# Stores of the last two groups' v tiles moved from SyncE's queue to ScalarE's, with the first exponentials and one wait reordered

## The chip, the cores and the metric

The kernel runs on one core of a Trainium2 chip. The metric is the device time of one execution in microseconds (us). TensorE is PE in the profile, VectorE is DVE, ScalarE is ACT, GpSimd is POOL, SyncE is SP. SP computes nothing here: it waits for semaphores and issues DMAs.

## The reference, cut to what matters

One block of a gated cross-attention model. Eight batches of 128 tokens, width 512, 32 heads of width 128 (so q, k and v are 4096 wide), then a mixture-of-experts feed-forward. Only the attention matters for this change:

```python
x = _rmsnorm(hidden_states, ln_weight)
h_q = (x @ w_q.T).reshape(b, lq, H, DH)
h_k = (key_value_states @ w_k.T).reshape(b, lk, H, DH)
h_v = (key_value_states @ w_v.T).reshape(b, lk, H, DH)
score = jnp.einsum('bqhd,bkhd->bhqk', h_q, h_k) + position_bias[None]
score = jnp.where(m, score, -jnp.inf)
score = jax.nn.softmax(score, axis=-1)
score = jnp.where(m, score, 0.0)
attn = jnp.einsum('bhqk,bkhd->bqhd', score, h_v).reshape(b, lq, H * DH)
return hidden_states + attn @ w_out.T
```

All matrices are float32. Products that need it are made of three float32r products each, from a high and a low part of both sides (`three`, L798 to L805).

## The kernel before

**Stages.** (1) Projections of k and q, two heads a step, 32 steps (`project_seven`), written to DRAM as `kq`. (2) v of head groups 0 to 5, in 12 steps (`project_v_seven`), from PSUM by way of `st` to DRAM as `v_all`; a group is four heads, 512 columns. Steps alternate between `kq_stored[0]` and `kq_stored[1]`; the last step, STEPS - 1, counts on `kq_stored[1]`. (3) Attention, a loop over 32 heads, i from 0 to 31, with group g = i // 4. (4) The feed-forward.

**v of groups 6 and 7** is made inside stage 3, as work between the heads: 16 tiles m, 128 tokens by 512 columns each (`project_v(m)`, 12 matmuls of 128x512 into `ps_job[m % 2]`). ACT copies a tile to `v_out[:, m % 2]` (`take_v(m)`) and SP stores it to `v_all` (`keep_v(m)`, L544 to L546). `v_out` has two places, so the copy of tile m waits until the store of tile m - 2 has landed (`v_kept[m % 2]`), and `project_v(m)` waits until tile m - 2 has left PSUM (`v_sbuf` at m - 1). Tiles 0 to 4 (AHEAD) come ahead of head 0; FILL gives tiles 5 to 7 to head 0, 8 to 10 to head 1, 11 to 13 to head 2 and 14, 15 to head 3.

**PE's order in stage 3** (L1036 to L1052): `score(0)`, tiles 0, 1, 2, `score(1)`, tiles 3, 4, and then for each i `turn_probs(i)`, `score(i + 2)`, `attend(i)`, and the tiles of FILL (from head 4 on, output projections instead).

**One head** passes through the engines so: PE `score(i)` in two halves of four batches; DVE `bias_and_max(i)` adds POOL's `score_bias` and takes the row maximum; ACT `exps(i, half)`, four exponentials with row sums; DVE `normalise(i, half)`; PE `turn_probs(i)` transposes; ACT `take_pT(i)` copies the transposes to `pT`; PE `attend(i)`, whose matmuls read `pT` and `v_s`; ACT `take_attn_hi(i)` and DVE `take_attn_lo(i)` take the result from PSUM. All the order is written by hand: each engine has one program, and an instruction waits behind all that stand ahead of it.

**ACT's order around the change.** Ahead of its first tile stands `act.wait_ge(kq_stored[(STEPS - 1) % 2], stores(STEPS - 1))`: the stores of the last step of stage 2 must have landed, since `pT` lies where `st` was. Then tiles 0, 1, exps(0, 0), tiles 2, 3, exps(0, 1), tile 4, exps(1, 0), exps(1, 1), and in each head `take_pT(i)`, exps(i + 2, 0), `take_attn_hi(i)`, one tile, exps(i + 2, 1), the other tiles.

**SP's order** in the loop over heads: loads of k and q of head i + 2 (`load_kq`, behind score(i)), its position bias, for i = 0 the last group's weights (`load_wv_last(1)`), for i = 1 `load_v(1)` (2 MB), for i = 2 `load_wo(0)` (1 MB), and then the stores of the tiles made at that head: five for i = 0, three for each of the next three, two for i = 4.

Of the kernel before, what the change touches and what calls it, by code (L numbers as in the profile page):

```python
# [32 lines left out]
B = 8  # L33
# [61 lines left out]
def stores(s):  # L95

    return 16 * ((s // 2 + 1) if s < KQ else KQ // 2 + 2 * ((s - KQ) // 2 + 1))
# [8 lines left out]
def build(nc, x, ctxT, mask, gains, pbias, lnw, wa, wv, wo, sw12, sw3, ew12, eb12, ew3, rw, rb, b3, out):  # L106
    with ExitStack() as stack:
# [358 lines left out]
        def _(sp):  # L466
# [74 lines left out]
                    sp.wait_ge(wo_split, g)  # L541
                sp.dma_start(wo_raw[g % 2][:], wo[g]).then_inc(wo_in, 16)

            def keep_v(m):  # L544
                sp.wait_ge(v_sbuf, m + 1)
                sp.dma_start(v_all[2 * PAIRS + m // B, m % B], v_out[:, m % 2]).then_inc(v_kept[m % 2], 16)  # L546

            sp.wait_ge(const_done, 1)
            for s in range(KQ):
                if s + 2 < KQ:  # L550
# [27 lines left out]
            for i in range(H):  # L578
                g, j = divmod(i, G)
                if i + 2 < H:  # L580
                    sp.wait_ge(score_psum, 2 * (i + 1))
                    load_kq(i + 2)
                    sp.wait_ge(bias_ready, i + 1)
                    load_pos(i + 2)
                if i == 0:
                    sp.wait_ge(wv_last_split, 1)
                    load_wv_last(1)
                if i == 1:
                    load_v(1)
                if i == 2:  # L590
                    load_wo(0)
                if i < G:
                    for m in (AHEAD, FILL[0], FILL[1], FILL[2])[i]:
                        keep_v(m)
                if i == G:
                    for m in FILL[3]:
                        keep_v(m)
                if j == 1 and 0 < g < NG - 1:
                    sp.wait_ge(attn_psum, 2 * G * g)
                    load_v(g + 1)  # L600
                if j == 2 and g:
                    if g == 1:
                        sp.wait_ge(v_psum, 2 * B)
                    else:
                        sp.wait_ge(o_psum, B * (g - 1))
                    load_wo(g)
                if i == H - G + 1:
                    sp.dma_start(x_res[:], x.rearrange("t p d -> p t d")).then_inc(x_res_in, 16)
# [682 lines left out]
        def _(act):  # L1291
            act.dma_start(w_raw[0][:, 3], wa[0, :, 3]).then_inc(first_w_in, 16)

            def copy(dst, src):
                return nc.scalar.activation(dst, src, ACT.Copy)  # L1295
# [14 lines left out]
            def take_v(m):  # L1310
                act.wait_ge(v_psum, m + 1)
                if m >= 2:
                    act.wait_ge(v_kept[m % 2], 16 * (m // 2))
                copy(v_out[:, m % 2], ps_job[m % 2][:]).then_inc(v_sbuf, 1)

            def high_wv(u, k):
                block, j = ORDER[k], 7 * u + k - HI_PLACES
# [12 lines left out]
            def take_pT(i):  # L1330
                for half in range(2):
                    act.wait_ge(pT_psum, 2 * i + 1 + half)
                    copy(pT[:, half], ps_turn[half][:]).then_inc(pT_sbuf, 1)
# [124 lines left out]
                        for k in ((), (0,), (2,), (4, 5))[n]:  # L1458
                            high_wv(u + 1, k)

            act.wait_ge(kq_stored[(STEPS - 1) % 2], stores(STEPS - 1))
            for m in AHEAD:
                take_v(m)
                if m in (1, 3):
                    exps(0, m // 2)
            exps(1, 0)
            for i in range(H):
                g = i // G
                if i == 0:
                    exps(1, 1)  # L1470
                take_pT(i)
                if i + 2 < H:
                    exps(i + 2, 0)
                take_attn_hi(i)
                if g == 0:
                    take_v(FILL[i][0])
                if i + 2 < H:
                    exps(i + 2, 1)
                if g == 0:
                    for m in FILL[i][1:]:  # L1480
                        take_v(m)


            def split_w12(n):
# [652 lines left out]
```

## Time and profile before

| what | value |
|---|---|
| median of 3 runs | 984.06 us (982.69, 984.06, 2479.74) |
| profiled execution | 979.98 us, of which span 978.2 us |
| mean granted TensorE clock | 0.994 |
| PE busy | 943.2 us, 96% of the span |
| DVE, ACT, POOL busy | 643.6 us, 410.9 us, 280.4 us |
| DMA | 193.75 MB, mean 198 GB/s |

The profile is of one execution. The span is from its first to its last instruction; the time is 1.8 us longer. A row of the timeline gives the start in us from the span's start, the duration, the engine, the line and the tile, and in brackets how long the engine sat idle before it and what ended that. Ends of matmuls are modelled, so a matmul's busy time laps over the next one's; distances between starts are to be read. "issue" names idle time for which the profile shows no releaser.

### The profile page before, as it was taken

The page shows a single profiled execution, that of the slowest core. Times are in us where ns is not written, and L with a number is a line of the kernel's source. Part 1 is how long each engine was busy: PE and PEld are TensorE (multiplying, and loading weights), DVE is VectorE, ACT ScalarE, POOL GpSimd, SP SyncE. Part 2 cuts the span into 40 slices and gives each one's busy share as a digit, 9 for nine tenths or more (in the row PEclk, how much of TensorE's full clock was granted, in tenths as well). Part 3 has the DMA queues.
Part 4 walks back from the last instruction along what each step waited for, and adds up shares of the span by engine and source line. Part 5 has one row for each costly group of instructions (what it writes and reads, how often), then busy time and mean ns, then how long its engine had stood idle before and what let it go on. Part 6 is the DMA issues. An engine that isn't in the chain of part 4 may idle for free.

```text
span 978.2 us, 13972 instructions
## 1 busy us (share of the span) xinstructions
PE 943.2 (96%) x4843; PEld 786.7 (80%) x4843; DVE 643.6 (66%) x1068; ACT 410.9 (42%) x1004; POOL 280.4 (29%) x252
## 2 busy tenths in 40 slices
PE   7999999999999899997999999999999999989994
PEld 6888888888888688886889898988989887767772
DVE  6877679666665765643768777787787777843331
ACT  6236553333332342212655455554554425324442
POOL 1253424342433323002122222221221012043364
PEclk9999999999999999999999999999999999999998
DMA  7655554655547525637747737456365049565579
GB/s 267 212 198 180 191 186 151 226 194 182 211 166 250 202 111 191 216 134 261 274 157 286 244 108 265 166 193 221 133 226 184 38 180 334 201 205 175 173 181 253
DMA packets 86787, 193.75 MB, mean 198 GB/s; under 512 B 8608, under 2 KB 29344, under 8 KB 85312
## 3 DMA queue, kind: packets, MB, share of 16 engines
q1 hardware_dynamic: 79312, 177.67, 51.1%
q0 software_dynamic: 4784, 12.58, 5.6%
q10 hardware_dynamic: 2624, 2.62, 0.8%
q8 instruction: 40, 0.66, 0.3%
q14 instruction: 27, 0.22, 0.1%
HBM read 121.74 MB, written 71.11 MB: 197 GB/s over the span
## 4 chain that ended last, share of the span: by engine, by line
PE 59%; DVE 4%; DMA 1%; issue 1%; ACT 1%; another core or an unknown queue 0%; DVEq 0%; SPq 0%; ACTq 0%
PE ps_job L802 7%; PE ps_job L804 6%; PE ps_job L803 6%; PE ps_attn L1016 6%; PE ps_score L988 6%; PE ps_attn L1251 5%; PE ps_turn L1002 3%; PE ps_job L1260 3%; PE ps_turn L1235 1%; PE ps_attn L933 1%; PE ps_attn L932 1%; PE ps_attn L930 1%; DMA v_all<-st 1%; PE ps_score L930 1%; PE ps_score L933 1%; PE ps_score L932 1%
## 5 line engine op out<-in xcount | busy, mean ns | idle before, releaser
L726 POOL TENSOR_TENSOR score_bias<-mask_bias,pos_bias 128x1024 f32<-128x1024 f32 x32 | 78.0, 2436 | 300.2 <-DVE probs L1801 198.1
L1305 ACT ACTIVATE probs<-probs,neg_max 128x128 f32<-128x128 f32 x256 | 99.5, 392 | 97.4 <-DVE neg_max L1804 97.4
L685 POOL TENSOR_TENSOR w_sum<-w_raw 128x256 f32<-128x256 f32 x30 | 22.7, 758 | 179.6 <-PE ps_score L864 72.3
L1016 PE MATMUL ps_attn<-pT,v_s 128*128 128x128 f32 x512 | 62.6, 275 | 1.5 <-issue 1.2
L1251 PE MATMUL ps_attn<-ew_s,xbT 128*128 x248 | 62.1, 380 | 0.9 <-ACT xbT L1295 0.9
L988 PE MATMUL ps_score<-kq_s 128*128 128x128 f32 x512 | 62.4, 275 | 0.0
L1016 PEld LDWEIGHTS ps_attn<-pT,v_s 128*128 128x128 f32 x512 | 59.8, 192 | 1.9 <-issue 1.4
L1251 PEld LDWEIGHTS ps_attn<-ew_s,xbT 128*128 128x128 f32 x248 | 44.6, 190 | 20.4 <-issue 15.0
L988 PEld LDWEIGHTS ps_score<-kq_s 128*128 128x128 f32 x512 | 59.8, 192 | 0.2
L1801 DVE TENSOR_TENSOR probs<-ps_score,score_bias 128x512 f32<-128x512 f32 x64 | 43.7, 683 | 23.2 <-PE ps_score L988 20.6
L1828 DVE TENSOR_TENSOR acc<-ps_job,acc 128x512 f32<-128x512 f32 x56 | 37.9, 686 | 29.6 <-PE ps_job L804 29.6
L758 POOL DMA_INDIRECT xb<-x_rows,token_of x31 | 31.2, 1008 | 85.5 <-ACT y_out L1557 38.1
L1295 ACT ACTIVATE w_hi<-w_sum 128x1024 fp32r<-128x1024 f32 x30 | 31.8, 1061 | 53.1 <-POOL w_sum L690 53.1
L1295 ACT ACTIVATE w_hi<-w_raw 128x768 fp32r<-128x768 f32 (+3 forms) x38 | 31.2, 822 | 54.0 <-PE ps_score L864 24.0
L1295 ACT ACTIVATE pT<-ps_turn 128x512 f32<-128x512 f32 x64 | 34.5, 592 | 45.6 <-PE ps_turn L1002 45.6
L802 PE MATMUL ps_job<-wo_hi,attn_even_lo 128*128 128x512 f32 x128 | 51.2, 400 | 0.0
L1648 DVE TENSOR_TENSOR w_lo<-w_raw,w_hi 128x768 fp32r<-128x768 f32 (+1 forms) x31 | 41.0, 1323 | 14.6 <-ACT w_hi L1295 14.2
L804 PE MATMUL ps_job<-wo_hi,attn_even_hi 128*128 128x512 f32 x128 | 50.0, 391 | 0.0
L803 PE MATMUL ps_job<-wo_lo,attn_even_hi 128*128 128x512 f32 x128 | 49.9, 389 | 0.0
L1305 ACT ACTIVATION_READ_ACCUMULATOR probs<-probs,neg_max 128x1 f32 x256 | 48.8, 191 | 0.0
L1815 DVE TENSOR_TENSOR probs<-probs,row_scale 128x512 f32<-128x512 f32 x64 | 44.3, 692 | 2.2
L1804 DVE TENSOR_REDUCE neg_max<-probs 128x4 f32<-128x512 f32 x64 | 43.9, 686 | 2.2
(465 smaller groups left out, 2596.6 us busy)
## 6 DMA issues: line engine op xcount, KB each, us to landing
kq<-st SPq DMA_DIRECT2D x32, 1024.0 KB, 4.2
kq_s<-kq SPq DMA_DIRECT2D x64, 512.0 KB, 4.5
v_s<-v_all SPq DMA_DIRECT2D x8, 2048.0 KB, 10.8
w_raw<-wa_dram SPq DMA_DIRECT2D x31, 512.0 KB, 5.6
v_all<-st SPq DMA_DIRECT2D x24, 512.0 KB, 3.7
y_slots<-ones SPq DMA_DIRECT2D x32, 256.0 KB, 4.7
wo_raw<-wo_dram SPq DMA_DIRECT2D x8, 1024.0 KB, 6.8
ew_s<-ew_dram SPq DMA_DIRECT2D x4, 2048.0 KB, 12.8
```

Source lines behind the costliest of these rows:

```text
L726: nc.gpsimd.tensor_tensor(score_bias[:], mask_bias[:], pos_bias[:, i % 2].unsqueeze(1).broadcast_to([P, B, P]), ALU.add).then_inc(bias_rea ...
L802: nc.tensor.matmul(psum, l_lo, r_hi, start=(k == 0), stop=False)
L803: nc.tensor.matmul(psum, l_hi, r_lo, start=False, stop=False)
L804: last = nc.tensor.matmul(psum, l_hi, r_hi, start=False, stop=(closed and k == n - 1))
L988: last = nc.tensor.matmul(ps_score[half][:, cols(b)], kq_s[:, i % 2, 1, tok], kq_s[:, i % 2, 0, tok], start=True, stop=True)
L1016: last = nc.tensor.matmul(ps_attn[half][:, cols(b)], v_s[g % 2][:, BH * half + b, cols(j)], pT[:, half, cols(b)], start=True, stop=True)
L1251: last = nc.tensor.matmul(ps_attn[k][:, 0:2 * P], xbT[k][:, cols(c)], ew12_s[:, e, c], start=(c == 0), stop=(c == C - 1))
L1295: return nc.scalar.activation(dst, src, ACT.Copy)
L1305: last = nc.scalar.activation(probs[i % 2][:, half, b], probs[i % 2][:, half, b], ACT.Exp, bias=neg_max[:, i % 2, half, b:b + 1], accum_ou ...
L1801: V.tensor_tensor(probs[i % 2][:, half], ps_score[half][:].rearrange("p (b k) -> p b k", b=BH), score_bias[:, BH * half:BH * (half + 1)], ...
L1804: V.tensor_reduce(neg_max[:, i % 2, half], probs[i % 2][:, half], AX.X, ALU.max, negate=True)\
L1815: V.tensor_tensor(probs[i % 2][:, half], probs[i % 2][:, half], row_scale[:, half].unsqueeze(2).broadcast_to([P, BH, P]), ALU.mult).then_i ...
```

## The change

SP's `keep_v` and its calls go. `take_v` on ACT now waits for its own copy and issues the store itself. The wait for `kq_stored[1]` moves behind the five tiles ahead, to just before the first `take_pT`. The exponentials stand otherwise: exps(0, 0) behind tile 1 and exps(0, 1) behind tile 2, exps(1, 1) behind `take_pT(0)`, exps(2, 0) behind tile 5 and exps(2, 1) behind tile 7. Two waits for all stores stand ahead of `take_attn_hi(6)`.

```diff
-            def keep_v(m):
-                sp.wait_ge(v_sbuf, m + 1)
-                sp.dma_start(v_all[2 * PAIRS + m // B, m % B], v_out[:, m % 2]).then_inc(v_kept[m % 2], 16)
...
-                if i < G:
-                    for m in (AHEAD, FILL[0], FILL[1], FILL[2])[i]:
-                        keep_v(m)
-                if i == G:
-                    for m in FILL[3]:
-                        keep_v(m)
...
                 copy(v_out[:, m % 2], ps_job[m % 2][:]).then_inc(v_sbuf, 1)
+                act.wait_ge(v_sbuf, m + 1)
+                act.dma_start(v_all[2 * PAIRS + m // B, m % B], v_out[:, m % 2]).then_inc(v_kept[m % 2], 16)
...
-            act.wait_ge(kq_stored[(STEPS - 1) % 2], stores(STEPS - 1))
             for m in AHEAD:
                 take_v(m)
-                if m in (1, 3):
-                    exps(0, m // 2)
+                if m in (1, 2):
+                    exps(0, m - 1)
             exps(1, 0)
+            act.wait_ge(kq_stored[(STEPS - 1) % 2], stores(STEPS - 1))
             for i in range(H):
                 g = i // G
+                take_pT(i)
                 if i == 0:
                     exps(1, 1)
-                take_pT(i)
-                if i + 2 < H:
+                elif i + 2 < H:
                     exps(i + 2, 0)
+                if i == G + 2:
+
+                    for n in range(2):
+                        act.wait_ge(v_kept[n], 16 * B)
                 take_attn_hi(i)
                 if g == 0:
                     take_v(FILL[i][0])
-                if i + 2 < H:
+                if i == 0:
+                    exps(2, 0)
+                elif i + 2 < H:
                     exps(i + 2, 1)
                 if g == 0:
                     for m in FILL[i][1:]:
                         take_v(m)
+                if i == 0:
+                    exps(2, 1)
```

ACT's program before, from its first copy of a v tile (`probs_73` is `probs` of even heads, `probs_74` of odd ones; each pair of `probs` rows is one exps of four exponentials):

```order
L1295 ACTIVATE v_out<-ps_job 128x512 [waits v_psum,kq_stored1]
L1295 ACTIVATE v_out<-ps_job 128x512 [waits v_psum]
L1305 ACTIVATE probs_73,row_sum<-probs_73,neg_max 128x128 [waits max_done]
L1305 ACTIVATE probs_73,row_sum<-probs_73,neg_max 128x128 x3
L1295 ACTIVATE v_out<-ps_job 128x512 [waits v_kept0,v_psum]
L1295 ACTIVATE v_out<-ps_job 128x512 [waits v_kept1,v_psum]
L1305 ACTIVATE probs_73,row_sum<-probs_73,neg_max 128x128 [waits max_done]
L1305 ACTIVATE probs_73,row_sum<-probs_73,neg_max 128x128 x3
L1295 ACTIVATE v_out<-ps_job 128x512 [waits v_kept0,v_psum]
L1305 ACTIVATE probs_74,row_sum<-probs_74,neg_max 128x128 [waits max_done]
L1305 ACTIVATE probs_74,row_sum<-probs_74,neg_max 128x128 x3
```

ACT's program now, from the same place up to the copy and store of tile 3 (L1285 is now the line of the copy helper, L1306 the store's):

```order
L1285 ACTIVATE v_out<-ps_job 128x512 [waits v_psum]
L1306 DMA v_all<-v_out 128x512 [waits v_sbuf]
L1285 ACTIVATE v_out<-ps_job 128x512 [waits v_psum]
L1306 DMA v_all<-v_out 128x512 [waits v_sbuf]
L1295 ACTIVATE probs_73,row_sum<-probs_73,neg_max 128x128 [waits max_done]
L1295 ACTIVATE probs_73,row_sum<-probs_73,neg_max 128x128 x3
L1285 ACTIVATE v_out<-ps_job 128x512 [waits v_kept0,v_psum]
L1306 DMA v_all<-v_out 128x512 [waits v_sbuf]
L1295 ACTIVATE probs_73,row_sum<-probs_73,neg_max 128x128 [waits max_done]
L1295 ACTIVATE probs_73,row_sum<-probs_73,neg_max 128x128 x3
L1285 ACTIVATE v_out<-ps_job 128x512 [waits v_kept1,v_psum]
L1306 DMA v_all<-v_out 128x512 [waits v_sbuf]
```

The first copy no longer waits for `kq_stored1`, and a DMA stands behind each copy. Behind tile 7, at the end of head 0, ACT went straight to the copies to `pT` of head 1 before:

```order
L1295 ACTIVATE v_out<-ps_job 128x512 [waits v_kept0,v_psum]
L1295 ACTIVATE v_out<-ps_job 128x512 [waits v_kept1,v_psum]
L1295 ACTIVATE pT<-ps_turn 128x512 [waits pT_psum] x2
L1305 ACTIVATE probs_74,row_sum<-probs_74,neg_max 128x128 [waits max_done]
L1305 ACTIVATE probs_74,row_sum<-probs_74,neg_max 128x128 x3
```

Now the store of tile 7 and exps(2, 1) stand between:

```order
L1285 ACTIVATE v_out<-ps_job 128x512 [waits v_kept0,v_psum]
L1306 DMA v_all<-v_out 128x512 [waits v_sbuf]
L1285 ACTIVATE v_out<-ps_job 128x512 [waits v_kept1,v_psum]
L1306 DMA v_all<-v_out 128x512 [waits v_sbuf]
L1295 ACTIVATE probs_73,row_sum<-probs_73,neg_max 128x128 [waits max_done]
L1295 ACTIVATE probs_73,row_sum<-probs_73,neg_max 128x128 x3
L1285 ACTIVATE pT<-ps_turn 128x512 [waits pT_psum] x2
```

The two exponential rows there are exps(2, 1), which stood behind tile 5 before. SP's queue before, from the loads of head 2 (i = 0) to the stores of head 1:

```order
L522 DMA kq_s<-kq 128x1024 [waits kq_stored1,score_psum]
L522 DMA kq_s<-kq 128x1024
L525 DMA pos_bias<-pbias_dram 128x128 [waits bias_ready]
L516 DMA wv_last_raw_72<-wv_dram 128x2048 [waits wv_last_split]
L546 DMA v_all<-v_out 128x512 [waits v_sbuf] x5
L522 DMA kq_s<-kq 128x1024 [waits kq_stored1,score_psum]
L522 DMA kq_s<-kq 128x1024
L525 DMA pos_bias<-pbias_dram 128x128 [waits bias_ready]
L537 DMA v_s_61<-v_all 128x8x512 [waits v_in,kq_stored1,kq_stored0]
L546 DMA v_all<-v_out 128x512 [waits v_sbuf] x3
```

And now:

```order
L522 DMA kq_s<-kq 128x1024 [waits kq_stored1,score_psum]
L522 DMA kq_s<-kq 128x1024
L525 DMA pos_bias<-pbias_dram 128x128 [waits bias_ready]
L516 DMA wv_last_raw_72<-wv_dram 128x2048 [waits wv_last_split]
L522 DMA kq_s<-kq 128x1024 [waits kq_stored1,score_psum]
L522 DMA kq_s<-kq 128x1024
L525 DMA pos_bias<-pbias_dram 128x128 [waits bias_ready]
L537 DMA v_s_61<-v_all 128x8x512 [waits v_in,kq_stored1,kq_stored0]
L522 DMA kq_s<-kq 128x1024 [waits kq_stored0,score_psum]
```

The loads that stood behind five and then three stores now wait for the scores alone. PE's, DVE's and POOL's programs are unchanged.

## Rows read from the trace of the kernel before

**Rows 1.** Waits of PE from 439 us on: total us, times, longest.

```profile
PE ps_job L802 <- ACT v_out L1295: 5.2, 1, 5.2
...
PE ps_attn L1016 <- issue: 1.2, 1, 1.2
...
PE ps_turn L1002 <- DVE probs L1815: 0.2, 1, 0.2
```

**Rows 2.** Chain that ended last, 435 to 500 us: start, duration, what.

```profile
440.95 10.60 DMA v_all<-st
```

**Rows 3.** Timeline of ACT: start, duration, line, tile, idle before.

```profile
451.57 1.09 ACT L1295 ACTIVATE v_out<-ps_job 128x512 f32<-128x512 f32 x2 [13.92 <-DMA v_all<-st]
...
464.01 0.60 ACT L1295 ACTIVATE v_out<-ps_job 128x512 f32<-128x512 f32 x1 [0.59 <-PE ps_job L804]
...
466.04 0.39 ACT L1305 ACTIVATE probs<-probs,neg_max 128x128 f32<-128x128 f32 x1
...
467.58 1.06 ACT L1295 ACTIVATE pT<-ps_turn 128x512 f32<-128x512 f32 x2
...
478.51 0.60 ACT L1295 ACTIVATE v_out<-ps_job 128x512 f32<-128x512 f32 x1 [2.12 <-PE ps_job L804]
479.00 1.08 ACT L1295 ACTIVATE pT<-ps_turn 128x512 f32<-128x512 f32 x2
```

**Rows 4.** Timeline of PE, same columns: tiles ahead, head 0, head 1.

```profile
446.59 0.39 PE L804 MATMUL ps_job<-wv_last_hi,ctx_hi 128*128 128x512 f32 x1
452.22 0.79 PE L802 MATMUL ps_job<-wv_last_hi,ctx_lo 128*128 128x512 f32 x1 [5.24 <-ACT v_out L1295]
...
456.55 1.95 PE L988 MATMUL ps_score<-kq_s 128*128 128x128 f32 x16
458.25 0.47 PE L802 MATMUL ps_job<-wv_last_hi,ctx_lo 128*128 128x512 f32 x1
...
463.81 0.60 PE L1002 MATMUL ps_turn<-ident,probs 128*128 128x128 f32 x4
...
468.26 2.02 PE L1016 MATMUL ps_attn<-pT,v_s 128*128 128x128 f32 x16 [1.21 <-issue]
470.04 0.47 PE L802 MATMUL ps_job<-wv_last_hi,ctx_lo 128*128 128x512 f32 x1
...
478.31 1.03 PE L1002 MATMUL ps_turn<-ident,probs 128*128 128x128 f32 x8
...
480.97 1.95 PE L1016 MATMUL ps_attn<-pT,v_s 128*128 128x128 f32 x16
482.67 0.48 PE L802 MATMUL ps_job<-wv_last_hi,ctx_lo 128*128 128x512 f32 x1
```

**Rows 5.** Busy time by stretch: each engine, granted clock, DMA share, GB/s.

```profile
452.00:454.00 2.00, 1.78 (x4) 1.49 (x5) 0.00 (x0) 2.00 (x10) 0.00 (x0) 0.50 1.05 420
...
456.00:458.00 2.00, 2.00 (x17) 1.87 (x16) 0.29 (x1) 0.00 (x0) 0.00 (x0) 1.00 0.54 200
```

**Rows 6.** Tile v_out: the issues of its stores (ns), and issue to landing.

```profile
L546 SPq DMA_DIRECT2D v_all<-v_out x16: 319/320/327, 452.2 to 514.3; - x16
...
DMA to landing us min/median/max: 2.0/2.2/6.4
```

**Rows 7.** Timeline of SP's queue, 425 to 515 us.

```profile
441.56 1.11 SPq L522 DMA_DIRECT2D kq_s<-kq  x2
...
452.19 12.76 SPq L546 DMA_DIRECT2D v_all<-v_out  x5
...
466.50 0.37 SPq L537 DMA_DIRECT2D v_s<-v_all  x1
```

**Rows 8.** Line L522, the two loads issued from 441.6 us: issue to landing.

```profile
DMA to landing us min/median/max: 11.2/11.5/11.9
```

**Rows 9.** Line L1420, a 256 KB load on ACT's queue: issue (ns), landing.

```profile
L1420 ACTq DMA_DIRECT2D lnw_s<-lnw_dram x1: 477/477/477, 34.9 to 34.9; - x1
...
DMA to landing us min/median/max: 4.9/4.9/4.9
```

## The prediction

> **What bounds the kernel now.** I read the page first: PE is busy 96% of the span. So a change in ACT's program counts only where PE waits for ACT. The waits of PE from 439 us on, the start of stage 3, show few [rows 1]: one of 5.2 us for a copy to `v_out`, one of 1.2 us ahead of `attend(0)`, 0.2 us ahead of the second half of `turn_probs(0)`. The chain says what is behind the first: a store `v_all<-st` that takes 10.6 us to land, until 451.55 [rows 2]. ACT starts its first copy of a v tile at 451.57, after 13.9 us of idleness [rows 3], since it waits for `kq_stored[1]` first, though `v_out` has nothing to do with `st`. PE, with tiles 0 and 1 finished at 446.82 (446.59 and one matmul of 0.23), stands until 452.22 [rows 4]. Then it pays again: the granted clock is 0.50, the level of 1.2 GHz, from 452 to 454 us, and 1.00 from 456 on [rows 5]; tile 2 takes 456.55 - 452.22 = 4.33 us, where tiles 5 to 7 take (478.31 - 470.04) / 3 = 2.76 each [rows 4].
>
> Head 0 is slow as well. From the end of tile 4 to the first tile behind `attend` PE takes 470.04 - 463.81 = 6.23 us; in head 1 the same work takes 482.67 - 478.31 = 4.36 [rows 4]. The 1.87 us between come from exps(0, 1) and from exps(1, 0) and (1, 1), which stand ahead of `take_pT(0)`: copy of tile 4 at 464.01, copies to pT at 467.58 [rows 3].
>
> **The first wait goes: what it gives.** Tile 0 ends at about 446.82 - 2.76 = 444.06. Its copy now starts 0.20 later (the distance of 463.81 and 464.01, and of 478.31 and 478.51 [rows 3, 4]), long before PE asks for `ps_job[0]` at 446.82. PE then runs on: tile 2 to 449.58, `score(1)` for 1.70 (456.55 to 458.25) to 451.28, tiles 3 and 4 for 5.56 (458.25 to 463.81) to 456.84 [rows 4]. Before, it was 463.81: **6.97 us gained**, of which 5.40 is the standstill and 1.57 the slow clock (4.33 - 2.76).
>
> **What that rests on: store 0.** Copy 2 waits for store 0, and tile 4 waits for copy 2. Tile 4 would start at 456.84 - 2.78 = 454.06, and PE follows the start of a copy by 0.65 (451.57 to 452.22), so store 0 may land up to 453.4. It is issued 0.62 after the start of its copy (451.57 to 452.19 [rows 3, 7]), so at about 444.9, and has 8.5 us. Landing takes 2.2 us at the median and 6.4 at most, the latter for the stores issued at 452.2 behind all that SP had queued [rows 6, 7]. But at 444.9 more is queued than at 452.2: the transfers that SP has issued by then keep the DMA engines full (share 1.05, 420 GB/s) until 456 or so [rows 5], and the two issued at 441.56 took 11.2 and 11.9 us [rows 7, 8]. If ACT's queue is served beside SP's, store 0 (256 KB) lands in 2.2 to 5 us, which is the 4.9 us that a 256 KB load on ACT's queue took [rows 9]; if it is served in the order of issue over both queues, it lands where it lands now, at 452.2 + 6.4 = 458.6. The trace has no case that tells these apart; I take the first, since the rows of ACT's own queue are nearest, and keep the second as a rival.
>
> The Trainium skill (DMA: Bandwidth & Descriptors, Queues, rings and completion order) says that SP and ACT each have a ring of their own on every DMA engine and that an engine goes round its rings packet by packet. By that rule store 0 passes the backlog, and the sum is as here; the 4.9 us of rows 9 agree but do not prove it. The same page (Issuing engines are not separate DMA queues) says that issuing from several engines saves only the sequencer's issue time; read strictly it speaks against this change and would give the time of the late store below.
>
> Stores 1 to 4 have more room: copy 3 waits for store 1 (issued at 447.6) and matters to tile 5 after 462; copy 5 waits for store 3 by 465.
>
> **What the stores cost ACT.** Each take_v now ties up ACT for longer: 0.62 from the copy's start to the issue, then the issue itself, 0.32 (SP, the same transfer [rows 6]) to 0.48 (ACT's queue [rows 9]). I take 0.40: the next instruction starts 1.02 behind the copy's start instead of 0.49 (478.51 to 479.00 [rows 3]). Sixteen times 0.53 is 8.5 us, nearly all under ACT's idleness; it counts where pT waits. There are two such places.
>
> - Head 0. From the end t of tile 4: copy t + 0.20, store to t + 1.22, exps(1, 0) 4 x 0.385 (466.04 to 467.58 [rows 3]) to t + 2.76, `pT`, and `attend(0)` 0.68 later (467.58 to 468.26 [rows 3, 4]) at t + 3.44. PE is ready at t + 2.66 (478.31 to 480.97). It waits 0.78; the 0.42 ahead of it goes, as exps(0, 1) ends at about 452.4 now and DVE has normalised by 457. Head 0 takes 4.36 + 0.78 = 5.14 instead of 6.23: **1.09 gained**.
> - Head 1. exps(2, 1) now stands between store 7 and `take_pT(1)`: the same 3.44 against 2.66, where no wait was: **0.78 lost**.
>
> With the issue at 0.32 or 0.48 each wait is 0.70 or 0.86. Heads 2 and 3 have a store but no exps ahead of pT: t + 1.90, hidden.
>
> **Edits at nothing.** The moved wait: its store landed at 451.55, and pT is not wanted before 459. If it were later by 1.9 us (three stores of 256 KB at 420 GB/s) it would still be hidden; queued behind it are the copies to pT. The waits at head 6 are for stores some 25 us old; behind them stand `take_attn_hi(6)` and all ACT does, but nothing is late. SP's loads come sooner: `load_v(1)`, issued at 466.50 before [rows 7], now follows `score(1)`, at about 453. The loads of k and q for head 2 landed by 441.56 + 11.9 = 453.5 [rows 7, 8], plus 1.9 is 455.4, and `score(2)` wants them after 456.84: hidden by 1.4 us or more. Behind head 4 nothing changes, and PE has no other waits for ACT there, so what is gained stays to the end.
>
> **Sum.** 6.97 + 1.09 - 0.78 = 7.28 us. The profiled execution took 979.98 us (span 978.2 and 1.8 around it): **972.7**. The median of the runs shown lies 4.08 above the profiled one: 984.06 - 7.28 = **976.8**, which I predict. Extreme prices: with both waits of pT at 0.86, 0.16 less gain; with neither, 8.84 us, or 975.2. Further down is only the scatter between executions, up to 4.08 us.
>
> **The rivals**
> - **Late store.** Store 0 lands at 458.6. Copy 2 and tile 4 (459.2) come then; PE has stood 5.2 us, nearly as now, and pays the slow clock: tile 4 ends at 459.2 + 4.33 = 463.6 instead of 463.8. The stall has only moved from tile 2 to tile 4. Gain 0.2 + 0.31 = 0.5 us: 983.5. For: full DMA engines. Against: rows 9, and 8.5 us of room. Anything between gives 977 to 983.
> - **Starved stores, slower.** If ACT's queue gets nothing while SP's has work, the earlier loads hurt: 1 MB for head 3 and the 2 MB of `load_v(1)`, issued by 453 into a queue that is not yet empty. At 420 GB/s they take 7.3 us: store 0 lands at 465.9, tile 4 starts at 466.5 and ends at 470.8, 7.0 later than before. Less 0.31 that is 6.7 us slower: 990.8. It decides from a landing at about 459 on. Against: again rows 9, a load on ACT's queue amid SP's traffic.
> - **Dear issues.** If an issue on ACT takes two or three times 0.48, each of the two waits grows by 0.5 to 1.0: 978 to 979. Or the loads for `score(2)` slip past 456.84 by 1 or 2 us: the same times.
>
> **Numbers.** The case forecast 0.74, late store or in part 0.15, starved 0.03, dear issues or late loads 0.08. The range 972 to 983.5 leaves out the starved case and part of the scatter; the forecast's own is 973 to 979. A measurement of this kernel tells about 2%, 20 us, from no change; no case reaches that. Faster by over 2% 0.01, within 2% 0.98, slower by over 2% 0.01.
>
> **What would show it.** Right: ACT's first copy near 444.3; PE without a gap between tiles 1 and 4; granted clock 1.00 from 440 to 460; store 0 landing in under 8.5 us; gaps of about 0.8 us ahead of `attend(0)` and `attend(1)`; the first `turn_probs` near 456.8; ACTq issues of 0.3 to 0.5 us. Wrong: a PE gap ahead of tile 4 (late store), ahead of `score(2)` (late loads), gaps well over 0.8 ahead of the attends (dear issues), or a loss behind head 4.

## The result and the profile after

The kernel after takes 978.63 us at the median of 9 runs (977.05 to 980.71); the kernel before, run beside it, 983.0 (one of its nine runs took 2479.74 us and is left out of the ratio). The ratio is 0.9957, with a 95% interval of 0.9949 to 0.9966: about 4.4 us faster, where 7.28 were forecast. 978.63 lies in the range of 972.0 to 983.5, 1.8 us above the 976.8 predicted. That distance flatters the forecast: 976.8 was counted down from 984.06, the median of the first three runs of before. From 983.0, the median of all nine, 7.28 less is 975.7, and the kernel after is 2.9 us above that. The profiled execution took 978.93 us (span 977.2, mean granted clock 0.990), only 1.05 us less than the profiled execution of before; the reason is told below.

**The first wait is gone, as forecast.** PE's timeline of after, as in [rows 4]:

```profile
455.96 1.04 PE L992 MATMUL ps_turn<-ident,probs 128*128 128x128 f32 x8
...
462.65 2.90 PE L1006 MATMUL ps_attn<-pT,v_s 128*128 128x128 f32 x16 [3.86 <-issue]
...
474.34 1.03 PE L992 MATMUL ps_turn<-ident,probs 128*128 128x128 f32 x8
...
477.73 2.05 PE L1006 MATMUL ps_attn<-pT,v_s 128*128 128x128 f32 x16 [0.56 <-ACT pT L1285]
...
487.81 1.04 PE L992 MATMUL ps_turn<-ident,probs 128*128 128x128 f32 x8
```

The first `turn_probs` starts at 455.96 instead of 463.81. Measured from the start of `score(0)`, which came 0.82 us earlier in this execution, it is 17.20 us instead of 24.23: 7.03 gained, 6.97 forecast. The granted clock is 1.00 from 440 to 462 us. But `attend(0)` now waits 3.86 us, and `turn_probs(1)` is 474.34 - 455.96 = 18.38 us behind `turn_probs(0)`, where it was 14.50 before [rows 4] and 13.41 was forecast. Head 1, from `turn_probs(1)` to `turn_probs(2)`, takes 13.47 instead of 12.63. From there on the two kernels run alike: from `turn_probs(2)` to the last one it is 297.84 us before and 297.86 after. The waits of PE from 435 us on (total, times, longest; the first and fifth row of the view), as in [rows 1]:

```profile
PE ps_attn L1006 <- issue: 3.9, 1, 3.9
...
PE ps_attn L1006 <- ACT pT L1285: 0.8, 2, 0.6
```

**What `attend(0)` waits for.** "issue" names no releaser. ACT's timeline of after, as in [rows 3], shows it:

```profile
443.48 0.60 ACT L1285 ACTIVATE v_out<-ps_job 128x512 f32<-128x512 f32 x1 [6.64 <-PE ps_job L794]
444.11 0.35 ACTq L1306 DMA_DIRECT2D v_all<-v_out  x1
...
451.71 0.60 ACT L1285 ACTIVATE v_out<-ps_job 128x512 f32<-128x512 f32 x1 [2.85 <-DMA v_all<-v_out]
452.33 0.33 ACTq L1306 DMA_DIRECT2D v_all<-v_out  x1
...
454.27 0.58 ACT L1285 ACTIVATE v_out<-ps_job 128x512 f32<-128x512 f32 x1
454.88 0.33 ACTq L1306 DMA_DIRECT2D v_all<-v_out  x1
459.43 0.60 ACT L1285 ACTIVATE v_out<-ps_job 128x512 f32<-128x512 f32 x1 [4.58 <-DMA v_all<-v_out]
...
461.98 1.05 ACT L1285 ACTIVATE pT<-ps_turn 128x512 f32<-128x512 f32 x2
```

ACT's first copy is at 443.48 and store 0 is issued at 444.11. Copy 2 waits 2.85 us for that store to land, which costs PE nothing. Store 2, issued at 452.33, goes out of the same place of `v_out`. Copy 4, at 459.43, waits 4.58 us for it. exps(1, 0) and the copies to `pT` (461.98) stand behind copy 4 on ACT, and `attend(0)` follows at 462.65. PE had tile 4 done at 455.96, and ACT would have started copy 4 at 456.16 (0.20 later): it is 3.27 us late. With the 0.56 us of wait that head 1 shows without a late copy, that is 3.83 of the 3.86. Tile v_out of after, as in [rows 6]: the issues of its stores, and the landings of all 16:

```profile
L1306 ACTq DMA_DIRECT2D v_all<-v_out x16: 326/326/347, 444.1 to 511.2; - x16
...
DMA to landing us min/median/max: 2.0/4.0/7.5
```

Line L1306 of after, store 0 alone:

```profile
DMA to landing us min/median/max: 7.5/7.5/7.5
```

The same line, store 2 alone:

```profile
DMA to landing us min/median/max: 7.0/7.0/7.0
```

The median of 16 is 4.0 us, against 2.2 before; the first took 7.5 and the third 7.0. And the standstill costs a second time, as the first one did in [rows 5]. Stretches of after: each engine, granted clock, DMA share, GB/s:

```profile
460.00:462.00 2.00, 0.00 (x0) 0.00 (x0) 0.00 (x0) 1.60 (x10) 0.00 (x0) 1.00 1.06 403
462.00:464.00 2.00, 1.35 (x10) 1.38 (x11) 1.03 (x3) 2.00 (x9) 0.00 (x0) 0.90 1.05 406
464.00:466.00 2.00, 2.00 (x10) 1.90 (x9) 1.33 (x4) 1.46 (x6) 0.00 (x0) 0.50 1.06 410
466.00:468.00 2.00, 2.00 (x8) 1.55 (x8) 1.93 (x4) 0.19 (x1) 0.23 (x1) 0.75 1.05 413
```

PE does nothing from 460 to 462; the clock then is 0.50, the level of 1.2 GHz, from 464 to 466, and partly so on both sides. Head 0 takes 18.38 us where 13.41 were forecast, 4.97 more. By distances between starts, `attend(0)` is 6.69 us behind `turn_probs(0)`, where 3.44 were forecast: 3.25 more for the wait. From there to `turn_probs(1)` it is 11.69 us, where 9.97 were forecast: 1.72 more for the slow clock (the same work takes 10.08 in head 1).

**The two profiled executions differ elsewhere too.** Their 1.05 us are 0.82 ahead of `score(0)`, 2.29 in stage 3 (from `score(0)` to the last head's `turn_probs`, 349.20 to 346.91), and 2.1 lost behind it (189.4 to 191.5 us), where the change touches nothing. The last goes with a fall of the granted clock near 850 us, to 0.86 from 850 to 860 and 0.96 in the 10 us before. The kernel before shows such a fall too, in two further profiles of itself. Stretch of before_again:

```profile
850.00:860.00 10.00, 9.37 (x43) 7.38 (x43) 4.60 (x11) 3.05 (x7) 4.32 (x4) 0.83 1.04 391
```

The same 10 us of the first profile of before (the execution whose rows the prediction reads), with the clock at 1.00:

```profile
850.00:860.00 10.00, 9.31 (x50) 7.54 (x51) 6.14 (x14) 3.06 (x7) 4.31 (x4) 1.00 1.04 383
```

The later profiles of before also have a stage 3 that is 0.9 us longer. The slow clock behind the first wait lasts longer in them: tile 2 takes 455.94 - 450.81 = 5.13 us, where the prediction's rows have 4.33. PE's timeline of before_again, start of tile 2 and of `score(1)`:

```profile
450.81 0.80 PE L802 MATMUL ps_job<-wv_last_hi,ctx_lo 128*128 128x512 f32 x1 [5.31 <-ACT v_out L1295]
...
455.94 1.95 PE L988 MATMUL ps_score<-kq_s 128*128 128x128 f32 x16
```

So the profiled execution of before, 979.98 us, was a quick one, 3 us below the median of 983.0. Against before_again, stage 3 of after is 3.2 us shorter, which is most of the 4.4 measured. The medians and ratios below rest on several executions each and do not lean on that one profile.

### The profile page after: what moved, and what is told of

The parts are those of the page before. It is cut to its first block, busy times and chain, and to the rows that moved or that the text cites. A ratio compares the mean times of both kernels' runs of the same rounds, so it can differ in the third digit from the quotient of the medians.

```text
span 977.2 us, 13973 instructions
## 1 busy us (share of the span) xinstructions
PE 945.3 (97%) x4843; PEld 788.5 (81%) x4843; DVE 635.9 (65%) x1068; ACT 412.1 (42%) x1004; POOL 279.2 (29%) x252
## 4 chain that ended last, share of the span: by engine, by line
PE 91%; DVE 4%; DMA 2%; issue 1%; ACT 1%; another core or an unknown queue 0%; ACTq 0%; SPq 0%; DVEq 0%
PE ps_job L792 7%; PE ps_job L794 7%; PE ps_job L793 7%; PE ps_attn L1006 6%; PE ps_score L978 6%; PE ps_attn L1241 5%; PE ps_score L852 3%; PE ps_score L854 3%; PE ps_score L853 3%; PE ps_turn L992 3%; PE ps_attn L852 3%; PE ps_attn L854 3%; PE ps_attn L853 3%; PE ps_job L1250 2%; PE ps_job L852 2%; PE ps_job L854 2%
## 5 line engine op out<-in xcount | busy, mean ns | idle before, releaser
L1285 ACT ACTIVATE pT<-ps_turn 128x512 f32<-128x512 f32 x64 | 34.5, 591 | 48.8 <-PE ps_turn L992 48.8
L1285 ACT ACTIVATE w_hi<-w_raw 128x768 fp32r<-128x768 f32 (+3 forms) x38 | 31.2, 822 | 54.3 <-PE ps_score L854 24.0
L1285 ACT ACTIVATE w_hi<-w_sum 128x1024 fp32r<-128x1024 f32 x30 | 31.8, 1061 | 52.8 <-POOL w_sum L680 52.8
L1801 DVE TENSOR_TENSOR probs<-ps_score,score_bias 128x512 f32<-128x512 f32 x64 | 43.7, 683 | 14.5 <-PE ps_score L978 11.9
L1648 DVE TENSOR_TENSOR w_lo<-w_raw,w_hi 128x768 fp32r<-128x768 f32 (+1 forms) x31 | 40.6, 1309 | 14.5 <-ACT w_hi L1285 14.3
```

## The experiments

All times of stage 3 are PE's, from the start of `score(0)`: `turn_probs(0)`, `turn_probs(1)`, and the last head's. The ratio is an estimate from all runs of the kernel and those of before beside it, with its 95% interval; it can differ a little from the quotient of the medians (for a3 that is 971.47 / 980.72 = 0.9906, and the ratio 0.9919). The medians come from several chips: before took 983.0 beside after, 980.72 beside a1 to a4, 982.74 beside after_again, a5, a6 and b2, and 982.2 beside c1 and c2. So kernels of different groups are to be compared by their ratios.

| kernel | first | second | last | wait ahead of attend(0), attend(1) | median, us | ratio |
|---|---|---|---|---|---|---|
| before, first profile | 24.23 | 38.73 | 349.20 | 1.21, 0 | 983.0 | 1 |
| before_again | 25.09 | 39.60 | 350.08 | 1.22, 0 | 981.63 (one run) | |
| before_third | 25.09 | 39.59 | 350.10 | 1.20, 0 | 981.84 (one run) | |
| after | 17.20 | 35.58 | 346.91 | 3.86, 0.56 | 978.63 | 0.9957 (0.9949 to 0.9966) |
| after_again | 17.21 | 35.39 | 346.75 | 3.67, 0.56 | 978.67 | 0.9962 (0.9945 to 0.9979) |
| a1_wait_only | 24.51 | 39.02 | 349.52 | 1.63, 0 | 980.75 | 0.9999 (0.9989 to 1.0009) |
| a2_stores_only | 25.38 | 40.42 | 350.86 | 1.21, 0 | 981.28 | 1.0001 (0.9991 to 1.0011) |
| a3_four_places | 17.21 | 30.70 | 341.99 | 0.61, 0.56 | 971.47 | 0.9919 (0.9903 to 0.9934) |
| a4_tile4_late | 17.21 | 29.83 | 344.16 | 0, 2.00 | 972.76 | 0.9920 (0.9907 to 0.9932) |
| a5_loads_held | 17.21 | 35.39 | 348.25 | 3.69, 1.92 | 978.71 | 0.9968 (0.9953 to 0.9983) |
| a6_exps_as_before | 17.20 | 37.27 | 347.76 | 2.74, 0 | 979.22 | 0.9968 (0.9952 to 0.9984) |
| c1_weights_held | 17.20 | 30.78 | 343.21 | 0.72, 1.66 | 975.37 | 0.9926 (0.9908 to 0.9944) |
| c2_wait_and_places | 17.21 | 33.52 | 343.99 | 1.77, 0 | 976.14 | 0.9932 (0.9909 to 0.9955) |
| b2_early_exps | 17.20 | 29.83 | 340.31 | 0, 0 | 972.75 | 0.9899 (0.9884 to 0.9914) |

The theory (A): the gain that is missing is lost where copy 4 waits for store 2. The rivals: (B) SP's loads, which come sooner in the changed kernel, slow the stores; (C) the gain is given back behind head 4.

**a1_wait_only: the moved wait by itself.** On the kernel before; the stores stay on SP's queue.

```diff
-            act.wait_ge(kq_stored[(STEPS - 1) % 2], stores(STEPS - 1))
             for m in AHEAD:
...
                 if i == 0:
                     exps(1, 1)
+                    act.wait_ge(kq_stored[(STEPS - 1) % 2], stores(STEPS - 1))
                 take_pT(i)
```

> The kernel before with the wait for kq_stored[1] moved to just ahead of take_pT(0), and nothing else: the stores stay on SP's queue, the exponentials as before. If the queue matters: store 0 is issued at about 445 behind all that SP has queued and lands near 458, so that the stall only moves from tile 2 to tile 4: 0 to 1.5 us faster than before, with an idle time of PE of about 4 to 5 us ahead of tile 4. If the queue does not matter (stores land alike from both): store 0 in about 7.5 us at 452, no stall ahead of tile 4, 3 to 5 us faster, as the whole change.

Nothing is gained (0.9999). The stall has moved from tile 2 to tile 4. PE's timeline of a1:

```profile
460.51 0.80 PE L802 MATMUL ps_job<-wv_last_hi,ctx_lo 128*128 128x512 f32 x1 [4.99 <-ACT v_out L1295]
```

And ACT's timeline of a1:

```profile
459.86 1.22 ACT L1295 ACTIVATE v_out<-ps_job 128x512 f32<-128x512 f32 x2 [9.41 <-DMA v_all<-v_out]
```

Line L546 of a1, the store issued at 446.3 alone:

```profile
DMA to landing us min/median/max: 13.4/13.4/13.4
```

Copy 2 waits 9.41 us for a store that lands after 13.4. This is the prediction's late store, and it comes true when the stores stay where they were.

**a2_stores_only: the stores by themselves.** On the kernel before, with the first wait where it was.

```diff
-                    for m in (AHEAD, FILL[0], FILL[1], FILL[2])[i]:
-                        keep_v(m)
...
                 copy(v_out[:, m % 2], ps_job[m % 2][:]).then_inc(v_sbuf, 1)
+                act.wait_ge(v_sbuf, m + 1)
+                act.dma_start(v_all[2 * PAIRS + m // B, m % B], v_out[:, m % 2]).then_inc(v_kept[m % 2], 16)
```

> The kernel before with the stores issued by ACT behind each copy, the first wait and the exponentials as before. Store 0 is issued at about 452.2 as in the kernel before, but on ACT's queue: if ACT's queue is served beside SP's, it lands in clearly less than the 6.4 us that it took there, if by order over both queues, in the same 6.4. The standstill of 5.2 us ahead of tile 2 stays. Time: within 1 us of the kernel before by all theories; over 1 us faster would mean that the stores alone bring a part of the gain.

Nothing again (1.0001). PE's timeline of a2:

```profile
452.88 0.79 PE L796 MATMUL ps_job<-wv_last_hi,ctx_lo 128*128 128x512 f32 x1 [5.42 <-ACT v_out L1289]
```

Tile v_out of a2, the store issued at 452.85 (store 0) alone:

```profile
DMA to landing us min/median/max: 5.9/5.9/5.9
```

Issued at the same point on SP's queue, it took 6.4 [rows 6, 7]. That is not clearly less, so a2 by itself doesn't tell the queues apart; 7.5 against a1's 13.4, for a store issued 5.4 us behind the start of `score(0)` in both, does. Neither half of the change brings anything, and only both together do (0.9968 in a6 below, where the exponentials stand as before): the wait's going makes room, and the quicker landing keeps the next wait from filling it.

**a3_four_places: no copy ahead waits for a store.** `v_out` gets four places; a copy waits for the store four tiles earlier.

```diff
-        v_out = place("v_out", [P, 2, D], F32, at_attn + 2 * T * 4)
+        v_out = place("v_out", [P, 4, D], F32, at_attn + 2 * T * 4)
...
-                if m >= 2:
-                    act.wait_ge(v_kept[m % 2], 16 * (m // 2))
-                copy(v_out[:, m % 2], ps_job[m % 2][:]).then_inc(v_sbuf, 1)
+                if m >= 4:
+                    act.wait_ge(v_kept[m % 4], kept_from[m % 4] + 16 * (m // 4))
+                copy(v_out[:, m % 4], ps_job[m % 2][:]).then_inc(v_sbuf, 1)
```

> The changed kernel with four places in v_out instead of two, so that copy m waits for store m - 4. Theory A (the missing gain is copy 4's wait for store 2, 4.6 us of ACT, 3.9 us of PE and the slow clock behind it): copy 4 follows tile 4 at once, attend(0) waits 0.8 us instead of 3.9, turn_probs(0) to turn_probs(1) takes 13.4 us instead of 18.4, and the time is 4 to 5.5 us below the changed kernel's, about 973.5. Theory B (the earlier loads of SP are what delays ACT or PE): attend(0) still waits 3 to 4 us, same time as the changed kernel. Theory C (the gain is made in stage 3 and given back in the feed-forward): stage 3 shortens or not, the time stays within 1 us.

0.9919, some 7.9 us, and 0.9919 against 0.9957 of after is 3.7 us more. The stores still land slowly (7.4 us at most), but nothing on the path waits for them. ACT's timeline of a3, copy 4:

```profile
456.79 0.60 ACT L1285 ACTIVATE v_out<-ps_job 128x512 f32<-128x512 f32 x1 [2.13 <-PE ps_job L794]
```

And PE's timeline, the two attends:

```profile
460.02 2.02 PE L1006 MATMUL ps_attn<-pT,v_s 128*128 128x128 f32 x16 [0.61 <-issue]
...
473.46 2.05 PE L1006 MATMUL ps_attn<-pT,v_s 128*128 128x128 f32 x16 [0.56 <-ACT pT L1285]
```

The waits of 0.61 and 0.56 come from copy, issue and four exponentials that stand in a row ahead of `pT` (b2 takes them away). Stage 3 is 4.9 us shorter than after's (8.1 shorter than before_again's).

**a4_tile4_late: the wait stays, but `pT` does not stand behind it.** Two places as in after; copy 4 goes behind exps(1, 1), so behind the first copies to `pT`.

```diff
-            for m in AHEAD:
+            for m in AHEAD[:-1]:
                 take_v(m)
...
                     exps(1, 1)
+                    take_v(AHEAD[-1])
```

> The changed kernel, still with two places, but with the copy of tile 4 and its store behind take_pT(0) and exps(1, 1). Theory A: the wait for store 2 is off PE's path, attend(0) waits for nothing (exps(1, 0) is over before turn_probs(0)), turn_probs(0) to turn_probs(1) takes 12.6 to 13.4 us instead of 18.4: 4.5 to 6 us below the changed kernel. Theories B and C: within 1 us of the changed kernel.

Head 0 goes without a wait: `turn_probs(1)` at 29.83 instead of 35.58, so the whole wait of 3.86 and the slow clock were copy 4's. One head later it recurs: copy 7 waits 3.57 us for store 5, and the second copies to `pT` stand behind it. ACT's timeline of a4:

```profile
470.46 0.60 ACT L1285 ACTIVATE v_out<-ps_job 128x512 f32<-128x512 f32 x1 [3.57 <-DMA v_all<-v_out]
```

And PE's:

```profile
473.64 3.29 PE L1006 MATMUL ps_attn<-pT,v_s 128*128 128x128 f32 x16 [2.00 <-ACT pT L1285]
```

Of the 5.75 us, 3.0 are lost again there (head 1 takes 16.51 us, not 13.47). The ratio is 0.9920, some 3.6 us below after's 0.9957, where 4.5 to 6 were expected. Kernels a3 and a4 give the missing gain back in two unlike ways, and in both it comes back between `turn_probs(0)` and `turn_probs(1)`, so (A) is shown. Against before_again, stage 3 explains 5.9 of a4's 7.8 us. The clock near 850 stayed at 1.00 in a4's profile, and what follows the last `turn_probs` takes 187.9 us there, against 189.8 and 189.2 in a1 and a2 on the same chip, where it fell: that is the size of the rest. So a part of the ratios of a3 and a4 may be this clock and not the wait.

**a5_loads_held: the earlier loads put back.** SP's loads for head 3 and `load_v(1)` wait until tile 4 has been copied.

```diff
+                if i == 1:
+                    sp.wait_ge(v_sbuf, 5)
```

> The changed kernel, with SP's loads of head 3 and of v group 1 (3 MB) held until tile 4 has been copied, so that they are not in flight beside stores 0 to 3. If these earlier loads are what makes store 2 late, it lands in 2 to 4.5 us instead of 7, copy 4 waits 0 to 2 us, attend(0) waits 0.8 to 1.5, and 2 to 4 us are gained on the changed kernel. If the backlog issued up to 445 alone is what delays it, store 2 still takes 6 to 7 us and the time is the changed kernel's within 1 us. Store 0 takes 7 us in either case, as nothing of the loads was out before it landed.

Copy 4 waits as in after, and store 2 lands after 6.7 us instead of 7.0. ACT's timeline of a5:

```profile
458.83 0.60 ACT L1287 ACTIVATE v_out<-ps_job 128x512 f32<-128x512 f32 x1 [4.32 <-DMA v_all<-v_out]
```

Both are as expected if the earlier loads are not the cause. (B) falls: the loads issued from 450.7 to 452.1 are behind the traffic that delays store 2, not in it. Holding them only shifts them onto head 1, where copy 7 waits 3.49 us and `attend(1)` 1.92.

**c1_weights_held: the traffic that store 2 does meet.** The last group's weights (`load_wv_last(1)`, 1 MB, issued at 442.57 and landing after 16.4 us in after) wait until tile 4 has been copied, and with them all SP's loads behind them. Kernel a5, which holds only the latter, showed that these don't matter here.

```diff
+                    sp.wait_ge(v_sbuf, 5)
                     load_wv_last(1)
```

> The changed kernel, two places in v_out, with SP's load of the last group's weights (1 MB, issued at 442.6 in the changed kernel) held until tile 4 has been copied; all SP's loads behind it are held with it. If the landing of a store hangs on what SP has in flight when it is issued: store 0 still takes about 7 us (3 MB are ahead of it either way), but store 2, issued at 452.3, finds the queue nearly empty (5.1 MB less 1 MB, plus two stores, at 0.41 MB a us from 441.5 on leave 0.1 MB) and lands in 2 to 4 us; copy 4 waits 0 to 0.5 us, attend(0) 0.6 to 1.0 instead of 3.8, and the time is 3.5 to 5 us below the changed kernel, about 0.85% below the kernel before. If the 7 us are a property of ACT's queue whatever is in flight, store 2 takes 7 us again and nothing is gained.

Store 0, which meets stage 2's stores and the loads of k and q, still takes 7.6 us; store 2 lands after 3.8 instead of 7.0, copy 4 waits 1.35 (0 to 0.5 was expected), and 3.7 us come back in stage 3 (0.9926). ACT's timeline of c1:

```profile
456.40 0.60 ACT L1286 ACTIVATE v_out<-ps_job 128x512 f32<-128x512 f32 x1 [1.35 <-DMA v_all<-v_out]
```

PE's timeline of c1:

```profile
459.65 2.02 PE L1007 MATMUL ps_attn<-pT,v_s 128*128 128x128 f32 x16 [0.72 <-issue]
...
474.17 2.05 PE L1007 MATMUL ps_attn<-pT,v_s 128*128 128x128 f32 x16 [1.66 <-ACT pT L1286]
```

Line L1307 of c1, store 2 alone:

```profile
DMA to landing us min/median/max: 3.8/3.8/3.8
```

So most of store 2's lateness came from the 1 MB of weights on SP's queue. The held load then meets head 1: 1.66 us ahead of `attend(1)`.

**a6_exps_as_before: the other order of the exponentials.** After, with the exponentials where before had them.

```diff
-                if m in (1, 2):
-                    exps(0, m - 1)
+                if m in (1, 3):
+                    exps(0, m // 2)
...
-                take_pT(i)
                 if i == 0:
                     exps(1, 1)
-                elif i + 2 < H:
+                take_pT(i)
+                if i + 2 < H:
                     exps(i + 2, 0)
```

> The changed kernel with the exponentials in their old order (exps(0, 1) behind tile 3, exps(1, 0) and (1, 1) ahead of take_pT(0), exps(2, 1) behind tile 5). By the wait for store 2, pT(0) comes 1.55 us later than in the changed kernel (one more exps between copy 4 and pT), and head 1 gets its 0.6 us back: turn_probs(0) to turn_probs(1) about 18 to 20 us, 0.5 to 1.5 us slower in stage 3. If the reordering carried most of the gain instead, it is over 2.5 us slower and level with the kernel before.

exps(0, 1) is behind the late copy 3, and PE waits 2.64 us in the middle of `turn_probs(0)` and 2.74 ahead of `attend(0)`; without a wait ahead of `attend(1)`. Stage 3 is 0.85 us longer than after's. The ratios (0.9968, and 0.9957 and 0.9962 for after) have intervals that overlap, so the reordering is worth about 1 us in the profile, and the times don't resolve it.

**after_again, before_again, before_third: is the loss behind head 4 the kernel's?** No edits.

> The changed kernel once more, unchanged, for a second profile of it beside the others. If its lost gain is the wait for store 2, attend(0) again waits 3 to 4.5 us and store 0 and 2 again take about 7 us to land. If the feed-forward of the first profile, in which the granted clock fell for some us near 850 us, was a property of the execution and not of the kernel, the clock need not fall there, and the span is then 2 to 3 us shorter with the same stage 3. Time about 0.4 to 0.5% below the kernel before.

> The kernel before, unchanged, for a second profile. In all the other kernels the measured gain exceeds what stage 3 gives against the first profile of the kernel before by 0.4 to 2.8 us. If that first profile (979.98 us against a median of 983.0) was a lucky execution, the second shows stage 3 up to turn_probs(31) longer than 349.2 us, by 0.5 to 2 us, or the clock falling near 850 us, where it did not in the first, or both. If both are as in the first profile, the excess lies elsewhere and stays open.

> The same once more, for a third profile of the kernel before; the same is expected of it.

Both kernels show the fall of the clock near 850, and so does after_again, so that its span is not shorter; from the last `turn_probs` to the end it is 189.4 us in the first profile of before, 191.7 and 191.2 in the later ones, 191.5 and 191.1 in those of after. The second and third profile of before show what was expected of a lucky first one. (C) falls: nothing is given back there.

**c2_wait_and_places: without ScalarE's queue.** On the kernel before: the wait moved as in a1, `v_out` with four places as in a3, the stores left on SP's queue.

```diff
-                sp.dma_start(v_all[2 * PAIRS + m // B, m % B], v_out[:, m % 2]).then_inc(v_kept[m % 2], 16)
+                sp.dma_start(v_all[2 * PAIRS + m // B, m % B], v_out[:, m % 4]).then_inc(v_kept[m % 4], 16)
```

> The kernel before with the wait moved and four places in v_out, the stores still on SP's queue. If ACT's queue matters for the stores even with four places: store 0 lands 13 us after its issue as in the kernel with the wait alone, near 459 on the changed kernel's clock, copy 4 waits for it 2 to 3 us, exps(1, 0) and (1, 1) come behind, and stage 3 up to turn_probs(1) is 3 to 5 us longer than with four places on ACT's queue: 3 to 5 us below the kernel before. If only the number of places matters, it is level with four places on ACT's queue, 8 to 9 us below.

0.9932, where after has 0.9957. Store 0 takes 13.5 us here, and copy 4, which with four places waits for it, stands 2.41 us. ACT's timeline of c2:

```profile
458.19 0.60 ACT L1295 ACTIVATE v_out<-ps_job 128x512 f32<-128x512 f32 x1 [2.41 <-DMA v_all<-v_out]
```

Line L546 of c2, store 0 alone:

```profile
DMA to landing us min/median/max: 13.5/13.5/13.5
```

With the same four places a3 ends stage 3 at 341.99 and c2 at 343.99, and `turn_probs(1)` is 2.8 us later in c2, where 3 to 5 were expected. But the two differ in more than the queue: c2 has the exponentials in the old order, which made 0.85 us in a6, and no run has four places, ACT's queue and the old order. So the 2.0 us are queue and order together. The intervals of the two ratios overlap.

**b2_early_exps: what is left.** a3, with exps(1, 0) ahead of tile 4's copy and exps(2, 1) ahead of tile 7's, so that no issue stands between an exponential and `pT`.

```diff
+                if m == 3:
+                    exps(1, 0)
-            exps(1, 0)
...
                         take_v(m)
-                if i == 0:
-                    exps(2, 1)
+                        if m == 6:
+                            exps(2, 1)
```

> Four places in v_out, and the two exps ahead of pT moved into ACT's idle time: exps(1, 0) between the copies of tiles 3 and 4, exps(2, 1) between those of tiles 6 and 7. With the waits of attend(0) and attend(1) being exps ahead of pT (0.61 and 0.56 us in the four-place kernel), both go: turn_probs(0) to turn_probs(1) and on to turn_probs(2) take 12.6 us each, 1.7 us less than with four places alone in stage 3, so 1.0 to 1.2% below the kernel before. If other waits stand behind them, less than 0.5 us is gained.

No wait ahead of either attend; stage 3 is 1.7 us shorter than a3's, 9.8 shorter than before_again's, and the ratio is 0.9899, the lowest of this study and below both kernels (a3's interval overlaps with it; a3's lower median was measured on another chip, where before took 980.72). ACT's timeline of b2, where exps(1, 0) starts ahead of the copy of tile 4 and the copies to `pT` follow that copy's store:

```profile
455.37 0.40 ACT L1295 ACTIVATE probs<-probs,neg_max 128x128 f32<-128x128 f32 x1 [0.41 <-ACT v_out L1285]
...
457.09 0.60 ACT L1285 ACTIVATE v_out<-ps_job 128x512 f32<-128x512 f32 x1
457.72 0.33 ACTq L1306 DMA_DIRECT2D v_all<-v_out  x1
458.14 1.09 ACT L1285 ACTIVATE pT<-ps_turn 128x512 f32<-128x512 f32 x2 [0.46 <-PE ps_turn L992]
```

## Why the prediction was right and where it failed

- **First wait, 6.97 us: right** (7.03). The copy of tile 0 is 0.2 us behind PE, PE runs through tiles 1 to 4, the clock stays at 1.00.
- **"Stores 1 to 4 have more room": wrong, and this is the step that failed.** The prediction checked store 0 for copy 2, store 1 for copy 3 and store 3 for copy 5, and left out store 2 for copy 4, the one pair whose copy stands ahead of `pT`. At its own 5 us a landing that would have done no harm: copy 2 at 449.8, store 2 issued at 450.4 and landed by 455.4, copy 4 wanted at 457.0. The harm is in the limit that it drew. It gave store 0 until 453.4 us, 8.5 us in all; with copy 2 only then, store 2 is issued at 454.0, and 3.0 us are left for it. Two landings out of one place follow each other: from the first issue (444.11) to where copy 4 is wanted (456.16) there are 12.05 us, less 0.72 from the first landing to the second issue, so 11.3 us for both, or 5.7 each. They took 7.5 + 7.0 = 14.5. In c1, with 7.6 + 3.8 = 11.4, the wait is nearly gone.
- **Landing on ACT's queue, 2.2 to 5 us: wrong**, and the missed pair cost something only because of it (7.5, 6.0, 7.0, 6.4 for stores 0 to 3). The row it was drawn from, one load at 35 us [rows 9], met busy DMA engines as well (share 1.02 from 33 to 35 us), but a backlog that ended soon (0.74 from 37 to 40). The choice between "beside SP's queue" and "behind it" was half right: 7.5 against 13.4 in a1.
- **Head 0, 1.09 gained: wrong** in consequence (3.88 lost): 3.25 more of wait than forecast, 1.72 of slow clock, for which the forecast had nothing.
- **Head 1, 0.78 lost: right** (0.84; a wait of 0.56). The issue was put at 0.40 us and took 0.33; the next instruction starts 1.00 behind the copy's start, 1.02 forecast.
- **Edits at nothing: right.** ACT's copies to `pT` follow the exponentials without a gap (461.98), so the moved wait costs nothing; from `turn_probs(2)` on the two kernels take the same time, so the waits at head 6 don't either. The earlier loads cost nothing: a5 holds them and loses 1.3 us in stage 3 by it.
- **The sum in the profile.** 7.03 - 3.88 - 0.84 = 2.31 us in stage 3, where 7.28 was forecast. The time gained more, 4.4, since the profiled execution of before was a quick one. Against the later profiles of before 3.2 are explained, because the slow clock behind the first wait cost 0.8 us more there than the 1.57 of the forecast; the last 1.2 us stay open.
- **Rivals.** The late store, foreseen for store 0, came with store 2 instead: the same mechanism one pair later, at 3.3 us instead of 5.2. Its "anything between gives 977 to 983" holds the result, and so does the forecast's own 973 to 979. That 978.63 fell into the latter is partly luck, since head 0 went otherwise than forecast. Nothing starved, no issue was dear, no load was late.

## What to carry to other kernels

When a wait is taken away, work out every later use of the same buffer by its own chain (copy, issue, landing, copy, issue, landing), not the first one alone; with few places, landings add up. Two parts that bring nothing alone (a1, a2) can bring something together, and the larger part of the cure here was neither, but two more places. Take a landing time from a row with the same traffic around it, and take more than one profile of the kernel before if 2 or 3 us matter.

## What the runs showed of the hardware

**A store on a second queue waits for the backlog of the first, then shares.** Store 0 of after is issued at 444.11 us, while SP's transfers keep the DMA engines full. Queues of after (packets, MB, share of the 16 engines) from 446 to 448 us; q1 carries SP's transfers, q10 ACT's:

```profile
q1 hardware_dynamic: 383, 0.75, 99.0%
```

And from 448 to 450 us:

```profile
q1 hardware_dynamic: 279, 0.54, 69.9%
q10 hardware_dynamic: 134, 0.25, 32.7%
```

ACT's queue moves nothing until 448.0, 3.9 us after the issue, and then store 0 and store 1 together have 32.7% of the engines' time beside 69.9%. At about 410 GB/s, 3.9 us are 1.6 MB (an estimate from these rows). Store 2 of after, issued at 452.33, shows the same: ACT's queue moves one packet from 454 to 456 and 117 in the next 2 us. In a2, where store 0 is issued at 452.85, its first packets come between 456.0 and 456.3, when SP's transfers are nearly done. The quickest of after's 16 stores needs 2.0 us in all. The Trainium skill (DMA: Bandwidth & Descriptors, Queues, rings and completion order) says that an engine goes round its rings packet by packet, which would have let the store start at once; the trace agrees with the sharing but not with the start. What fills those 3.9 us, the runs don't show. The same page's sentence that issuing on several engines only saves issue time (Issuing engines are not separate DMA queues) does not hold here: 7.5 us against 13.4 (a1) for the same store.

**The granted clock near 850 us is in part a matter of the execution.** The same kernel before shows 1.00 in one profile and 0.83 in two. The profiles of a3, a4 and a5 show 1.00, and all others a fall between 840 and 860. It goes with 1.3 to 2.3 us between the last `turn_probs` and the end (189.4 against 191.7 and 191.2 for before; 187.6 and 187.9 for a3 and a4 against 189.8 and 189.2 for a1 and a2), a third to a half of what this change brought. Of 22 runs of before on one chip, three have a mean clock of 0.994 and take 979.75 to 980.13 us; the other 19 have 0.986 to 0.991 and take 980.79 to 986.53. Whether a kernel's own order makes the fall rarer, the runs don't show.
